# Reciprocal and division of a batch's output moved ahead of the row maximum of their slot on VectorE

## What is computed

```
x = x + tanh(g_xattn[0]) * attention(layernorm(x), ctx, ctx, Wq, Wk, Wv, Wo, bo)
x = x + tanh(g_ffn[0])   * experts(layernorm(x), controller, f1, bias, f2)

attention:
    scores = where(causal, Q @ K.T, -inf) / sqrt(D)       # per batch and head
    attn   = softmax(scores)                              # less the row maximum, exp, over the row sum
    out    = (attn @ V) @ Wo.T + bo
```

## Time and profile before

| | |
|---|---|
| median of 3 runs | 263.15 us |
| profiled execution, whole time | 263.96 us |
| its span | 262.2 us |
| TensorE matmul busy | 219.7 us, 84% |
| VectorE busy | 202.1 us, 77% |
| ScalarE busy | 166.3 us, 63% |
| GpSimd busy | 128.9 us, 49% |
| row maxima (L1267) | 64, 43.7 us, 682 ns each |
| reciprocals (L1275) | 16, 27.9 us, 1746 ns each |
| idle VectorE before row maxima | 14.8 us |

### The profile page before, as it was taken

How to read it: one execution, slowest core, us unless ns; L and a number is a source line. 1 busy time by engine, 2 the same in 40 slices (tenths; PEclk the granted TensorE clock), 3 DMA queues, 4 the chain that set the end, 5 groups by cost and what they waited for, 6 DMA issues and landing times.

```text
span 262.2 us, 7559 instructions
## 1 busy us (share of the span) xinstructions
PE 219.7 (84%) x2849; PEld 171.3 (65%) x2850; DVE 202.1 (77%) x472; ACT 166.3 (63%) x356; POOL 128.9 (49%) x243
## 2 busy tenths in 40 slices
PE   0474687798987999999899999969998999985992
PEld 0464576576765788787677777747776777872550
DVE  4896847789999699696899899999995555553563
ACT  2633766768667868596678775338786555546570
POOL 5652165658746767886487969446572000000000
PEclk9997979999999999999999999999999999998899
DMA  7747689931434344325220000018994587999723
GB/s 213 213 100 201 166 222 227 232 108 50 135 106 135 85 134 110 90 61 143 65 61 6 6 4 6 2 35 314 388 384 168 120 187 211 245 241 202 186 99 124
DMA packets 32231, 37.92 MB, mean 145 GB/s; under 512 B 4099, under 2 KB 27331, under 8 KB 31939
## 3 DMA queue, kind: packets, MB, share of 16 engines
q1 hardware_dynamic: 31661, 36.82, 50.9%
q10 hardware_dynamic: 534, 0.61, 0.8%
HBM read 18.26 MB, written 6.29 MB: 94 GB/s over the span
## 4 chain that ended last, share of the span: by engine, by line
PE 30%; DVE 19%; POOL 17%; issue 12%; DMA 11%; ACT 7%; SPq 3%; ACTq 0%; POOLq 0%; DVEq 0%
POOL pT L481 6%; DVE rsum L1275 4%; PE banks L731 4%; PE banks L753 4%; PE banks L930 3%; DMA y_rows<-ctrl 3%; PE banks L915 3%; PE banks L856 3%; DVE nmax L1267 3%; PE banks L602 3%; DMA y<-y_rows 2%; SPq L401 2%; DMA xs<-in_x_dram 2%; PE banks L711 2%; ACT pT L1022 2%
## 5 line engine op out<-in xcount | busy, mean ns | idle before, releaser
L481 POOL TENSOR_SCALAR_AFFINE_SELECT pT<-pT 128x512 f32<-128x512 f32 x64 | 40.8, 640 | 34.6 <-ACT pT L1022 34.3
L1267 DVE TENSOR_REDUCE nmax<-banks 128x4 f32<-128x512 f32 x64 | 43.7, 682 | 14.8 <-PE banks L665 14.7
L1027 ACT ACTIVATE banks<-cb 128x512 f32<-128x512 bf16 x62 | 37.0, 597 | 12.8 <-DVE nmax L1267 11.1
L1022 ACT ACTIVATE pT<-banks 128x512 f32<-128x512 f32 x64 | 37.5, 586 | 3.0 <-PE banks L682 2.9
L711 PE MATMUL banks<-pT,va 128*32 128x128 f32 x512 | 27.3, 285 | 0.9 <-POOL pT L481 0.8
L1275 DVE RECIPROCAL rsum<-banks 128x256 f32<-128x256 f32 x16 | 27.9, 1746 | 0.0
L665 PE MATMUL banks<-kst,qst 96*128 96x128 bf16 x256 | 25.4, 222 | 2.1 <-ACT banks L1027 2.1
L682 PE MATMUL banks<-qst,kst 99*128 99x128 bf16 x256 | 25.4, 221 | 1.2 <-DMA qst<-nT 1.0
L711 PE MATMUL banks<-pT,ones 128*32 128x128 f32 x512 | 25.7, 273 | 0.0
L1115 ACT ACTIVATE routed<-banks 128x512 f32<-128x512 f32 x30 | 17.2, 626 | 5.6 <-PE banks L753 5.6
L594 PE MATMUL banks<-cf,xn 128*128 128x128 f32 x32 | 6.0, 317 | 17.2 <-DVE xn L1220 14.2
(11 more groups left out here) (133 smaller groups left out, 624.4 us busy)
## 6 DMA issues: line engine op xcount, KB each, us to landing
wx<-in_wexp_dram SPq DMA_DIRECT2D x32, 256.5 KB, 8.1
kst<-kp SPq DMA_DIRECT2D x48, 128.0 KB, 2.6
qst<-qp SPq DMA_DIRECT2D x48, 128.0 KB, 2.4
cT<-in_ctxT_dram SPq DMA_DIRECT2D x8, 256.0 KB, 3.3
y_rows<-ring SPq DMA_DIRECT2D x16, 128.0 KB, 3.4
y<-y_rows SPq DMA_DIRECT2D x4, 512.0 KB, 5.3
wx<-y_rows SPq DMA_DIRECT2D x4, 512.0 KB, 8.8
out_dram<-xs SPq DMA_DIRECT2D x16, 128.0 KB, 1.9
```

The lines of the kernel that those rows point to most:

```text
L481: pool.affine_select(p, p, [[0, HC], [1, P]], ALU.is_ge, 0.0, base=0, channel_multiplier=-1)\
L1022: act.activation(pT[:, n % PR, :], BT[n % 2], ACT.Exp, scale=float(D) ** -0.5).then_inc(p_ready, 1)
L1027: act.activation(BS[n % 2], causal, ACT.Copy).then_inc(mask_placed, 1)
L1267: dve.tensor_reduce(nmax[:, b % 2, :].rearrange("p (e j o) -> p e o j", e=2, o=KH)[:, e, o], BS[n % 2].rearrange("p (j t) -> p j t", j=HC) ...
```

## The change

In the loop of VectorE the call of `weigh_out` stands ahead of `row_max(n)` instead of behind `row_max`, the normalizations, `k_rest`, `xT_low` and `q_rest` of its slot. It is still in the slots with n mod 4 = 2, still behind `residual` (which falls in other slots). The instructions themselves, their waits and all other engines are as they were.

```diff
                 s, g = n % 8, n // 8
                 if s % 4 == 0 and 0 <= (n - 20) // 4 < NB:
                     residual((n - 20) // 4)
+                if s % 4 == 2 and 0 <= n // 4 - 3 < NB:
+                    weigh_out(n // 4 - 3)
                 if n < CH:
                     row_max(n)
...
                 if s == 6 and g + 2 < NG2:
                     q_rest(g + 2)
-                if s % 4 == 2 and 0 <= n // 4 - 3 < NB:
-                    weigh_out(n // 4 - 3)
```

## The result

The changed kernel takes 274.21 us, the median of 4 runs (271.85 to 277.41), against 264.05 us for the kernel before on the same chip (4 runs, 263.0 to 266.31). The ratio is 1.038 with a 95% interval of 1.0323 to 1.0437: slower by about 10 us. The forecast was 269.0 us with a range of 265.0 to 272.5. The direction was right, but the measured time lies above the range, and the loss is about 4 us larger than I had worked out. The ratios here leave out executions in which the chip was disturbed, so they can differ from the ratio of the medians printed beside them, which are over all runs.

A forecast was written before the change was run, and what follows sets the result against it. VectorE was taken to bound the loop from 58 to 88 us, TensorE from 88 us on. The terms summed to +5.9 us on the median of 263.15, so 269.0 us, range 265.0 to 272.5.

The forecast's parts named there:

- Step 1: n = 34 and 42, TensorE-bound: late row maximum delays mask, `va` and projection by 2.04 us; +1.6 us each, +3.2 together.
- The bound above: Upper limit at n = 34 and 42: the full 2.04 us each, without the old wait of 0.47 us swallowed.
- Step 2: n = 26, end of the VectorE-bound stretch: same order of work and price as n = 34, +1.6 us.
- step 5: n = 14, 18, 22, VectorE-bound: late projections covered by TensorE's existing 1.31 us wait; +0.1 us, about 2.0 more without cover.
- Step 3: n = 30, 38, 46: VectorE's idle time hides the pair; 0, with up to 0.2 us each as the bound.
- Step 4: Earlier `on` where n mod 8 = 6: TensorE's waits at 129.41 and 130.42 us go, -1.1 us.
- Step 6: n = 50, 54, 58, 62, light slots: +1.5, +0.7, +0.2 and -0.3 us.
- Rival 1: Faster: waits for `on` are the real limit, TensorE's gaps close by 3.65 us, giving 259.5 us; chance 0.06.
- Rival 2: Absorbed, within 1%: a lead of 1.9 us halves the cost at the five full places; +2.4, some 265.5 us; chance 0.15.
- the five full places: n = 26, 34, 42, 50, 54, priced at 7.0 us together; half that price is 3.5 us less.
- Rival 3: Slower still: cover fails at n mod 8 = 6 and n = 14, 18, 22 isn't absorbed; about 275 us; chance 0.07.
- The signs to look for: Profile changes expected if right, among them `va` waits of about 2 us and 8-slot rounds 1.6 us longer from 88 to 122.

The follow-up runs named there:

- with filler: The changed kernel plus 8 matmuls that nobody reads in slots 19, 27, 35 and 43, while TensorE waits for `va`: 271.18 us, ratio 1.0269.

## Why the prediction was right and where it was wrong

The direction and the path of the loss were right. The size was wrong: 10 us in place of 5.9, because the sum had no term for the slower clock behind TensorE's new waits.

**What bounds the kernel, and the chain: right.** From 88 us on, TensorE's stream sets the pace, and the chain of row maximum, mask, `va`, projection has no slack at n = 34. It is shown by cutting it: with `va` ahead of the mask the ratio falls from 1.038 to 0.996.

**Step 1 (n = 34, 42; +1.6 each): the mechanism was right, the size half of the truth.** VectorE's pair took 2.13 us, the mask waited 1.96 us and TensorE 2.21 us, near the 2.04 worked out. (That figure ends the row maximum 0.60 us after its start, though its row shows 0.68; with 0.68 the mask moves by the whole 2.13. Against `kr` the projection moved by 2.07: 4.88 us after its start in place of 101.74 - 98.93 = 2.81.) For the wait alone 1.57 us was worked out, and 1.53 to 1.55 was measured wherever the clock stayed up (n = 34 in the kernel with n mod 8 = 2 alone, both places with filler). But 3.05 us was measured where it fell. **The term that failed is one that the sum didn't have**: all durations behind the wait were taken from rows at the full clock. The bound above (the full 2.04 us) could not hold it either, since it bounded the wait and not the speed of the work after it.

The Trainium skill (TensorE: Matmul & The Clock Gate, section HAM oscillation — how this bites in real kernels) describes a loop whose waits throttle TensorE again and again, so that the work behind each wait starts at half clock. The trace agrees on the mechanism: 1.72 us of full clock lost at each of four places. The waits in the page's example are about 3 to 5 us; here 2.21 us was enough, though not every time. The prediction had no rival in which new waits lower the clock.

**Step 2 (n = 26; +1.6): the right number by luck.** It measured 1.65, but only 0.22 with filler. I had taken the slot for a copy of n = 34. It isn't: in the kernel before, TensorE has three waits here, that of 1.31 us for `kr` and these two.

```profile
84.78 0.38 PE L624 MATMUL banks<-wh,onh 128*128 128x256 f32 x1 [0.34 <-ACT va L1014]
...
89.25 0.24 PE L694 MATMUL banks<-cb,npart 128*48 128x128 bf16 x1 [0.50 <-POOL npart L498]
```

In the changed kernel all three are gone, and one wait stands in their place:

```profile
84.69 0.60 PE L594 MATMUL banks<-cf,xn 128*128 128x128 f32 x4
...
88.52 0.58 PE L624 MATMUL banks<-wh,onh 128*128 128x256 f32 x1 [2.21 <-ACT va L1014]
...
93.84 0.24 PE L694 MATMUL banks<-cb,npart 128*48 128x128 bf16 x1
```

In waits that is 2.21 - 1.31 - 0.34 - 0.50 = 0.06 us, and the clock adds 1.72. The 1.31 us is the cover that I had named in step 5. Where n = 22 was early and n = 26 was not (mod 8 = 6 only, and n < 26 only), the place n = 26 gave back 1.32.

**Step 3 (n = 30, 38, 46; 0): right.** -0.01 and -0.02; the projections of slots 31, 39 and 47 don't wait.

**Step 4 (-1.1): right.** -1.06 at n = 46, and -1.05 with n mod 8 = 6 alone.

**Step 5 (n = 14, 18, 22; +0.1): failed.** The +0.1 was not added up from its parts: beside the -0.67 at n = 14 (-1.03 was measured) no price of n = 18 and 22 was given. It measured -1.03 + 1.86 + 1.13 = +1.96. With filler it is -0.68, and the return at n = 26 comes on top, so the cover holds for waits. It doesn't hold for a clock that falls behind a wait of over 3 us.

**Step 6 (n = 50 to 62; +1.5, +0.7, +0.2, -0.3, sum 2.1): right as a sum.** +0.70, +1.37, +0.48 and -0.60 make 1.95. The waits in slots 51, 55 and 59 are 1.15, 1.13 and 0.96 us, and the clock stays at 1.00.

**The sum.** In the kernel with filler the loop costs +3.50 us, so the terms of waiting were 5.9 - 3.5 = 2.4 us too high (1.4 in step 2, 0.8 in step 5), and the clock adds 7.07 that was in no term: 5.9 - 2.4 + 7.07 = 10.57. The error of the clock is the larger one, and that of the waits hid part of it.

**The rivals.** Rival 1 (faster) fell with all pairs early, but part of it is true at n mod 8 = 6: with the early pair there alone the ratio is 0.989 and the loop 0.46 us shorter, with `va` first as well 0.982 and 2.29 us. Rival 2 (half the price at the five full places) holds at none of the two that could be read by themselves: n = 34 and 42 cost 1.54 and 1.55 us with filler. Rival 3 named a time near 275, and 274.2 was measured, but not by its mechanism: step 3's cover held, and so did that of step 5 against the waits.

**The signs to look for.** The waits of about 2 us in slots 27, 35 and 43, the fall of the wait for `on`, and the waits gone at 129 to 130 us were as written. Two were not: a round of 8 slots from 88 to 122 us takes 3.0 us more and not 1.6, and VectorE's idle time before row maxima didn't fall (15.8 us against 14.8). It only moved: ahead of the row maximum of slot 37 VectorE now waits 1.99 us for TensorE's late scores.

## What to carry to other kernels

An instruction moved ahead on an engine without idle time delays the one that it passes; ask what is queued behind that one's consumer on each further engine until the engine that is the bound. Where that engine is TensorE, a new wait of about 2 us can have two prices, the wait and the slower clock behind it, which was as large here in the traces; give the second a rival of its own, since one wait of 2.21 us in this case cost nothing more. Split an edit of this kind by place: the same move cost 3.05 us in one kind of slot, nothing in the next and gave back 1.05 in another.

## What the runs showed of the hardware

- In this kernel a single wait of TensorE of about 2 us, in a loop in which it is otherwise busy, was mostly followed by a time at the lower clock (each kernel's trace is one execution). In the traces here TensorE waited 14 times for 1.99 to 3.23 us between 56 and 160 us, and the clock was below 1.00 behind 13 of them (1.72 us of full clock lost each time in the changed kernel). Behind three of the 13 twice as much was lost (3.4 us, n = 26 of the kernel with n mod 8 = 2 alone among them). TensorE waited 12 times for 1.31 to 1.52 us, and the clock fell behind one of them. So the price of a wait isn't certain in either direction: one of 2.21 us cost nothing more, and one of 1.31 us, which had been free before, cost 0.89.
- With matmuls that compute nothing in the wait, the clock stayed at 1.00 behind it and the place was cheaper by 1.5 us (3.05 to 1.55), although TensorE did more work. What they bring in whole time is smaller and not sure: a ratio of 1.027 in place of 1.038, with intervals that overlap.
- The clock also dips where nothing was changed, ahead of 54 us and behind 170 us in many of these traces. The granted clock of whole executions goes with their time: of the 72 executions of the kernel before, the 21 that were granted 0.975 or more took 263.6 us on average, the 8 below 0.960 took 267.7. So the dips are likely a part of the scatter of several microseconds between runs of one kernel; how large a part wasn't shown.
